# Stacks of split values filled by transfers within SBUF instead of through DRAM

## The chip, the cores and the metric

One core of a Trainium2 chip runs the whole program. The metric is the time of one execution on the device, in microseconds (us), lower is better; several runs are taken and their median stands.

## The reference

x is [16, 128, 256] and ctx_2048 is [16, 128, 256], both float32. Four layers follow each other, each added to x:

```python
x = x + _L0_xattn_ref(_layernorm(x, axis=-1), ctx_2048, ctx_2048)
x = x + _L0_ffn_ref(_layernorm(x, axis=-1), router_w, router_b, expert_w, expert_b)
x = x + _L1_xattn_ref(_layernorm(x, axis=-1), ctx_2048, mask_BxS2_bk0)
x = x + _L1_ffn_ref(_layernorm(x, axis=-1), w_r, b_r, w1, b1, w2, b2)
```

The first layer, which the change is about, cuts the 128 channels of each batch into 8 heads of 16. For each head it takes the 256 x 256 scores qk = q^T k / 4 (a contraction over 16 channels only), a softmax over the last axis, and the product with v, whose 16 channels of the head are the same ctx values as k. The second layer lets each of 16 experts take its 128 best tokens out of 2048 by a softmax of logits. The third is an attention over 128 masked memory tokens; a batch whose mask is all false gives zero. The fourth picks 64 of 128 tokens per batch and puts them through a feed-forward layer.

## The kernel before

Each engine has a program of its own, written out by hand, and they meet only at semaphores. The queue of SP issues nearly all transfers, in its program's order; ACT's queue issues only the small ones of neg_max.

**Units.** The first layer works in eight units (u) of two batches. A unit has 16 steps, one for each batch and head. A step is: scores (L1088 to L1097, PE), the maximum over each row of them (L527 to L532, DVE), the transposed scores with the maximum subtracted inside the product (scores_t, L1099 to L1110, PE), the exponential (L895, ACT), and after every fourth step the product with the values (L1112 to L1125). PE runs scores a good unit ahead of the exponentials: in unit 0 it does all 16 of unit 1 and the first 8 of unit 2. Unit 0's own scores and maxima come before that, from L1160 and L650. The row maxima are transposed (max_t), negated and split in two bf16 parts by ACT (neg_high) and DVE (neg_low), and sent by ACT's queue into two extra rows of q_stack (send_neg_max, L903); scores_t waits for them.

**Splits and stacks.** The scores need float32 accuracy out of bf16 products. So q and k are each split in three bf16 parts (high, mid, low: high is a cast, the rest is subtracted, mid is a cast of the rest, low what remains after it). q_stack and k_stack hold six rows of 16 channels each, with the parts so paired that one product over 96 partitions sums all six part products of a head. There are four slots, one per unit in flight. A stage load (load_stage, L222) brings two batches of ctx and x into ctx_stage and x_stage, 128 channels on 128 partitions. ACT casts (high_k L914, mid_k L920, high_q L924, mid_q L928); for units 0 and 1 DVE subtracts and scales (split_first, L491), for the later ones POOL subtracts (L334 to L350) and DVE scales (scale_q, L484). The head must move from the partition axis to the free axis, and that goes through DRAM: write_k_parts and write_q_parts (L233, L239) write six parts of 128 KB when k_split and q_split say so, and load_stacks (L245) reads them back when all six have landed: three transfers into k_stack and six into q_stack, each of these from 16 rows of 8 KB. PE waits for all nine (stacks_loaded).

**Order on SP** (L274 to L311): stage 0, mask, w_ones (the rows of ones in k_stack, L277), write the parts of 0, stage 1, stacks 0, write the parts of 1, stage 2, stacks 1; then, once the first neg_max has landed, load_x(0) and load_small (ten transfers of small weights); write the parts of 2, stage 3, stacks 2; then by unit: load_x, write parts of u+3, stage u+4, stacks u+3. A stage load waits until the stage before it has been transposed and split. high_k stands between the exponentials in ACT's program: before the first one for unit 2, after the ninth for unit 3, and later after the 14th of unit u for unit u+4.

**Also touched.** DVE computes constants (L508 to L523) after the split of unit 0, and from the mask the row mask_bias (L645) and valid (L646) ahead of the split of unit 1; of all these only high and low are used in the first layer. take_vt (L909) copies the transposed ctx to vt, which the third layer also uses.

## Time and profile before

| what | us |
|---|---|
| median of 3 runs | 420.14 |
| the runs | 419.99, 420.14, 425.96 |
| the profiled execution's own time | 422.43 |
| its span, first to last instruction | 420.2 |

A row of a timeline gives the start of a group of like instructions, the time from the first's start to the last's end, the engine and line, what it writes and reads, how many there are, and in brackets how long the engine had idled before it and who released it. SPq and ACTq are the queues that issue transfers: their time is that of issuing, not of the transfer. GB/s in a window is what all transfers of the core moved in it.

### The profile page before, as it was taken

How to read it: one execution, taken by the hardware profiler on the slowest of the kernel's cores; microseconds unless marked ns; L12 is line 12 of the kernel's file. 1: busy time of each engine (PE TensorE's matmuls, PEld its weight loads, DVE VectorE, ACT ScalarE, POOL GpSimd, SP SyncE). 2: the span in 40 equal slices, each digit the busy share in tenths (PEclk: the TensorE clock that was granted, in tenths of full speed). 3: DMA queues.
4: the chain of work that ended last, by engine and by line, in shares of the span. 5: the costliest groups of instructions: out<-in, count | busy, mean ns of one | idle time of the engine just before them, and what ended most of it. 6: DMA issues, size and time to landing. Idle time of an engine off the chain costs nothing.

```text
span 420.2 us, 7370 instructions
## 1 busy us (share of the span) xinstructions
PE 279.6 (67%) x1872; PEld 182.5 (43%) x1872; DVE 317.7 (76%) x989; ACT 167.6 (40%) x397; POOL 94.8 (23%) x222
## 2 busy tenths in 40 slices
PE   1134777777886877877778621001559999999996
PEld 0011333353442544444334310000438988888884
DVE  5847458899989889799986748888377888787631
ACT  4110543464654536464556500000111566445631
POOL 1101323352415224111111110000133322333200
PEclk9999975789698886899989965555555999999999
DMA  2789388959294581740000380000000000000001
GB/s 88 202 189 153 98 221 187 166 150 165 71 197 79 145 126 54 146 80 1 2 1 2 100 301 0 1 0 2 1 0 0 2 25 25 25 0 25 26 27 51
DMA packets 24379, 32.90 MB, mean 78 GB/s; under 512 B 4066, under 2 KB 22434, under 8 KB 22818
## 3 DMA queue, kind: packets, MB, share of 16 engines
q1 hardware_dynamic: 23842, 32.48, 33.5%
q10 hardware_dynamic: 512, 0.13, 0.2%
q8 instruction: 10, 0.16, 0.2%
q14 instruction: 15, 0.12, 0.1%
HBM read 24.02 MB, written 8.39 MB: 77 GB/s over the span
## 4 chain that ended last, share of the span: by engine, by line
DVE 35%; PE 33%; issue 12%; DMA 8%; ACT 4%; POOL 3%; SPq 2%; DVEq 1%; ACTq 1%; POOLq 0%
DVE row_max L531 7%; PE t_bank L1355 5%; PE pv_bank L1273 5%; PE pv_bank L1121 4%; DMA q_stack<-q_parts_dram 4%; DVE denom_inv L549 3%; PE score_bank L1094 3%; PE scoret_bank L1107 3%; PE t_bank L1150 2%; PE score_bank L1336 2%; DMA q_parts_dram<-q_parts 2%; ACT probs L895 2%; DMA q_stack<-neg_max 2%; PE score_bank L1303 2%; DVE junk L705 1%
## 5 line engine op out<-in xcount | busy, mean ns | idle before, releaser
L895 ACT ACTIVATE probs<-scoret_bank 128x512 f32<-128x512 f32 x128 | 73.1, 596 | 52.5 <-PE scoret_bank L1107 42.3
L531 DVE TENSOR_REDUCE row_max<-score_bank 128x2 f32<-128x512 f32 x112 | 74.4, 679 | 24.3 <-PE score_bank L1094 23.1
L1107 PE MATMUL scoret_bank<-q_stack,k_stack 98*128 98x256 bf16 (+1 forms) x256 | 54.6, 301 | 28.1 <-ACT probs L895 18.7
L1094 PE MATMUL score_bank<-k_stack,q_stack 96*128 96x256 bf16 (+1 forms) x240 | 53.6, 314 | 19.1 <-DMA q_stack<-q_parts_dram 11.0
L355 POOL TENSOR_SCALAR var_eps<-mv 128x1 f32<-128x1 f32 x48 | 9.2, 192 | 189.5 <-DVE mv L567 106.9
L1107 PEld LDWEIGHTS scoret_bank<-q_stack,k_stack 98*128 98x128 bf16 (+1 forms) x256 | 24.2, 104 | 46.6 <-ACT probs L895 20.5
L1121 PE MATMUL pv_bank<-probs,values_ones 128*32 128x256 f32 x512 | 42.0, 455 | 1.0 <-ACT probs L895 1.0
L1094 PEld LDWEIGHTS score_bank<-k_stack,q_stack 96*128 96x128 bf16 (+1 forms) x240 | 21.7, 105 | 47.8 <-issue 15.3
L1273 PE MATMUL pv_bank<-q_stack,k_stack 128*128 (+1 forms) x256 | 36.0, 285 | 0.4 <-ACT q_stack L1070 0.4
L1045 ACT COPY xnt<-score_bank 128x256 f32<-128x256 f32 x16 | 6.0, 373 | 74.6 <-PE score_bank L1294 74.6
L1273 PEld LDWEIGHTS pv_bank<-q_stack,k_stack 128*128 128x128 f32 x256 | 33.9, 202 | 1.3 <-issue 0.9
L1355 PE MATMUL t_bank<-k_stack,probs 128*128 128x256 f32 x128 | 29.4, 382 | 0.0
L357 POOL TENSOR_TENSOR rstd<-var_eps,minus_half 128x1 f32<-128x1 f32 x48 | 26.1, 543 | 8.8 <-POOL var_eps L355 8.8
L549 DVE RECIPROCAL denom_inv<-denom 128x256 f32<-128x256 f32 x16 | 27.7, 1732 | 0.0
L1355 PEld LDWEIGHTS t_bank<-k_stack,probs 128*128 128x128 f32 x128 | 23.7, 190 | 2.9
L1254 PE MATMUL t_bank<-count,same_expert 128*128 128x3 bf16 x15 | 2.8, 187 | 31.4 <-DVE equal L705 31.4
L1150 PE MATMUL t_bank<-wr_moving,xnt 128*128 128x272 f32 x64 | 22.0, 474 | 1.2 <-ACT xnt L943 1.2
L1064 ACT ACTIVATE probs<-pv_bank,b1s 128x128 f32<-128x128 f32 x64 | 17.6, 379 | 11.8 <-PE pv_bank L1273 11.7
L1121 PEld LDWEIGHTS pv_bank<-probs,values_ones 128*32 128x32 f32 x512 | 15.0, 122 | 16.2 <-issue 9.0
L1144 PE MATMUL t_bank<-ident,xn 128*128 128x128 f32 x32 | 7.0, 303 | 18.5 <-DVE xn L573 10.2
L1137 PE MATMUL t_bank<-ident,ctx_stage 128*128 128x128 f32 x32 | 7.6, 383 | 16.3 <-DMA x_stage<-in_x_dram 16.3
L1150 PEld LDWEIGHTS t_bank<-wr_moving,xnt 128*128 128x128 f32 x64 | 13.4, 234 | 8.1 <-issue 4.1
(182 smaller groups left out, 534.5 us busy)
## 6 DMA issues: line engine op xcount, KB each, us to landing
q_stack<-q_parts_dram SPq DMA_DIRECT2D x48, 128.0 KB, 6.9
k_parts_dram<-k_parts SPq DMA_DIRECT2D x24, 128.0 KB
q_parts_dram<-q_parts SPq DMA_DIRECT2D x24, 128.0 KB
k_stack<-k_parts_dram SPq DMA_DIRECT2D x8, 384.0 KB, 4.6
ctx_stage<-in_ctx_dram SPq DMA_DIRECT2D x8, 256.0 KB, 3.2
x_stage<-in_x_dram SPq DMA_DIRECT2D x8, 256.0 KB, 3.9
k_stack<-k_parts_dram SPq DMA_DIRECT2D x8, 256.0 KB, 5.3
xs<-in_x_dram SPq DMA_DIRECT2D x8, 256.0 KB, 7.3
```

The source lines that it names most:

```text
L355: pool.tensor_scalar(work, variance, EPS, factor, ALU.add, ALU.mult).then_inc(s[summed], 1)
L357: pool.tensor_tensor(dst, work, minus_half[:, 0:dst.shape[1]], ALU.pow).then_inc(s[ready], 1)
L531: dve.tensor_reduce(row_max[:, i, :, h], score_bank[bank_of][:, :].rearrange("p (m n) -> p m n", m=2), AX.X, ALU.max).then_inc(s["max_done ...
L549: dve.reciprocal(denom_inv[:, i, :], denom[:, i, :]).then_inc(s["div_step"], 1)
L895: act.activation(probs[:, j % PROBS, :], scoret_bank[j % 2][:, :], ACT.Exp).then_inc(s["exp_done"], 1)
L1064: act.activation(hid[:, h, :], hid_bank[h // 4][:, (h % 4) * P:(h % 4 + 1) * P], ACT.Gelu_apprx_tanh, bias=b1s[:, h:h + 1]).then_inc(s["f_ ...
L1094: ins = pe.matmul(to[:, m * D:(m + 1) * D], q_stack[0:QROWS, slot, h, b_in, m * P:(m + 1) * P], k_stack[0:QROWS, slot, h, b_in, :], start= ...
L1107: ins = pe.matmul(scoret_bank[j % 2][:, k * D:(k + 1) * D], k_stack[0:SROWS, slot, h, b_in, k * P:(k + 1) * P], q_stack[0:SROWS, slot, h, ...
L1121: ins = pe.matmul(pv_bank[i][pair * Q:(pair + 1) * Q, odd * D:(odd + 1) * D], values_ones[:, i, k, pair, odd, :], probs[:, (j - GROUP + 1 ...
L1150: ins = pe.matmul(t1_bank[:, 0:D + NE], xnt[:, i, k, :], wr_moving[:, k, :], start=(k == 0), stop=(k == 1))
L1273: ins = pe.matmul(hid_bank[h // 4][:, (h % 4) * P:(h % 4 + 1) * P], w1s[:, k, h * P:(h + 1) * P], zg[:, k, bass.ds(P * t, P)], start=(k == ...
L1355: ins = pe.matmul(y_bank[:, 0:D], hid[:, h, :], w2s[:, h, :], start=(h == 0), stop=(h == NF - 1))
```

## The change

It takes the two DRAM tensors out. A stage load now puts channel h * 16 + d on partition d * 8 + h (x_split, ctx_split), so that eight neighbouring partitions hold the eight heads of one d. A part on 128 partitions can then be copied to 16 partitions by 8 heads in the order in which both are walked. Each part goes to its place in the stack by a transfer of 128 KB within SBUF: six into k_stack (stack_k) and six into q_stack (stack_q), each group as soon as its part is ready (k_high, k_mid, k_split and so on) instead of after all. A stage load is now four transfers of 128 KB instead of two of 256 KB.

Unit 1 gets its own stage and part buffers, laid over the first six slots of probs, the tile of the exponentials; so stage 1 is loaded right behind stage 0, and ACT waits, before its first exponential, for all that still reads them. DVE's split of units 0 and 1 is cut in pieces: stats_q(1) goes into the split of unit 0, rest_k(1) and scale_q(1) follow the constants, and low_k(1), rest_q(1) and low_q(1) stand between the first five maxima. Unit 1's ctx transposes move behind PE's second score step.

Of the rest: the mask is loaded after the stacks of unit 1; mask_bias is computed by ACT after the exponential of the logits; valid by DVE in the third layer, after the first two c_scale; eight of the constants become more_constants, behind the subtraction of the logits' maxima. take_vt writes vt in channel order, a copy with a stride.

Left out below: the helpers that choose the buffer for unit 1 (ctx_staged, x_staged, k_parts_of, q_parts_of), the same waits on high_q, and POOL's waits for unit 1's splits ahead of unit 2's.

```diff
-        q_parts_dram = nc.dram_tensor("q_parts_dram", (NU, 3, C, NH, 2 * D), BF16, kind="Internal").ap()
-        k_parts_dram = nc.dram_tensor("k_parts_dram", (NU, 3, C, NH, 2 * D), BF16, kind="Internal").ap()
...
+        ctx_stage1 = probs[:, 0, :].rearrange("p (b n) -> p b n", b=2)
+        x_stage1 = probs[:, 1, :].rearrange("p (b n) -> p b n", b=2)
+        k_parts1 = probs[:, 2:4, :].rearrange("p s n -> p (s n)").bitcast(BF16)[:, 0:6 * D].rearrange("p (a n) -> p a n", a=3)
+        q_parts1 = probs[:, 4:6, :].rearrange("p s n -> p (s n)").bitcast(BF16)[:, 0:6 * D].rearrange("p (a n) -> p a n", a=3)
...
+        def wait_staged(eng, u):
+            if is_n(u, 0) or is_n(u, 1):
+                eng.wait_ge(s["staged1" if u else "staged"], 64)
+            else:
+                eng.wait_ge(s["staged"], 64 * u)
...
+            x_split = x.rearrange("b (h d) n -> d h b n", h=NH)
+            ctx_split = ctx_2048.rearrange("b (h d) n -> d h b n", h=NH)
+
             def load_stage(u):
-                if not is_first(u):
-                    sp.wait_ge(s["ctx_t"], u)
-                    sp.wait_ge(s["k_split"], u)
-                    sp.wait_ge(s["q_split"], u)
-                sp.dma_start(ctx_stage[:, :, :], ctx_rows[:, bass.ds(2 * u, 2), :]).then_inc(s["staged"], 16)
-                sp.dma_start(x_stage[:, :, :], x_rows[:, bass.ds(2 * u, 2), :]).then_inc(s["staged"], 16)
+                if not is_first(u) and not is_n(u, 1):
+                    before = 1 if is_n(u, 2) else u
+                    sp.wait_ge(s["ctx_t"], before)
+                    sp.wait_ge(s["k_split"], before)
+                    sp.wait_ge(s["q_split"], before)
+                signal = s["staged1" if is_n(u, 1) else "staged"]
+                for i in range(2):
+                    sp.dma_start(ctx_staged(u)[:, i, :], ctx_split[:, :, bass.ds(2 * u + i, 1), :]).then_inc(signal, 16)
+                for i in range(2):
+                    sp.dma_start(x_staged(u)[:, i, :], x_split[:, :, bass.ds(2 * u + i, 1), :]).then_inc(signal, 16)
...
-            def write_k_parts(u):
-                sp.wait_ge(s["k_split"], u + 1)
-                for part in range(3):
-                    sp.dma_start(k_parts_dram[u, part].rearrange("d h n -> h d n"),
-                                 k_parts[:, part, :]).then_inc(s["parts_written"], 16)
...
-            def load_stacks(u, reused):
-                slot = u % SLOTS
-                wait_apart(sp, s["parts_written"], 96 * (u + 1))
...
+            def stack_k(u, reused):
+                rows = k_stack[:, u % SLOTS].rearrange("p h b n -> p h (b n)")
                 if not is_first(u):
-                    wait_apart(sp, s["stacks_loaded"], 144 * u)
+                    wait_apart(sp, s["k_stacked"], 96 * u)
                 if reused:
                     wait_apart(sp, s["scorest_ready"], STEPS * (u - SLOTS + 1))
-                k_rows = k_parts_dram[u].rearrange("p d h n -> (p d) (h n)")
-                q_rows = q_parts_dram[u].rearrange("p d h n -> p d (h n)")
-                part_of_row = (0, 0, 0, 1, 1, 2)
-                k_to = k_stack[:, slot].rearrange("p h b n -> p (h b n)")
-                q_to = q_stack[:, slot].rearrange("p h b n -> p (h b n)")
-                sp.dma_start(k_to[0:3 * C], k_rows).then_inc(s["stacks_loaded"], 16)
-                sp.dma_start(k_to[3 * C:5 * C], k_rows[0:2 * C]).then_inc(s["stacks_loaded"], 16)
-                sp.dma_start(k_to[5 * C:6 * C], k_rows[0:C]).then_inc(s["stacks_loaded"], 16)
-                for row in range(6):
-                    sp.dma_start(q_to[row * C:(row + 1) * C], q_rows[part_of_row[row]]).then_inc(s["stacks_loaded"], 16)
+                for part, signal, places in ((0, "k_high", (0, 3, 5)), (1, "k_mid", (1, 4)), (2, "k_split", (2,))):
+                    wait_apart(sp, s[signal], u + 1)
+                    for n in places:
+                        sp.dma_start(rows[n * C:(n + 1) * C], k_parts_of(u)[:, part, :]).then_inc(s["k_stacked"], 16)
+
+            def stack_q(u):
+                rows = q_stack[:, u % SLOTS].rearrange("p h b n -> p h (b n)")
+                if not is_first(u):
+                    wait_apart(sp, s["q_stacked"], 96 * u)
+                for part, signal, places in ((0, "q_high", (0, 1, 2)), (1, "q_mid", (3, 4)), (2, "q_split", (5,))):
+                    wait_apart(sp, s[signal], u + 1)
+                    for n in places:
+                        sp.dma_start(rows[n * C:(n + 1) * C], q_parts_of(u)[:, part, :]).then_inc(s["q_stacked"], 16)
...
             load_stage(0)
-            sp.dma_start(mask_u8[:, :, :], mask.rearrange("(a b) m -> a b m", a=1).to_broadcast([P, NB, P])).then_inc(s["mask_loaded"], 16)
+            load_stage(1)
             sp.wait_ge(s["ones_done"], 1)
             sp.dma_start(k_stack[QROWS:SROWS].rearrange("p s h b n -> p (s h) (b n)"),
                          ones_bf[:, :].unsqueeze(1).to_broadcast([2, SLOTS * NH, 2 * D])).then_inc(s["w_ones"], 16)
-            write_k_parts(0)
-            write_q_parts(0)
-            load_stage(1)
-            load_stacks(0, False)
-            write_k_parts(1)
-            write_q_parts(1)
+            stack_k(0, False)
+            stack_q(0)
             load_stage(2)
-            load_stacks(1, False)
+            stack_k(1, False)
+            stack_q(1)
+            sp.dma_start(mask_u8[:, :, :], mask.rearrange("(a b) m -> a b m", a=1).to_broadcast([P, NB, P])).then_inc(s["mask_loaded"], 16)
             sp.wait_ge(neg_loaded[0], 32)
             load_x(0)
             load_small()
 
-            write_k_parts(2)
-            write_q_parts(2)
+            stack_k(2, False)
+            stack_q(2)
             load_stage(3)
-            load_stacks(2, False)
...
             stats_q(0)
-            split_first(0)
+            rest_k(0)
+            dve.tensor_copy(ident_bf[:, :], ident[:, :])
             link(dve.tensor_scalar(earlier[:, :], free_f[:, :], part_f[:, 0:1], None, ALU.is_lt))
-            dve.tensor_copy(ident_bf[:, :], ident[:, :])
-            link(dve.tensor_scalar(work_i[:, :], free_i[:, :], 15, None, ALU.bitwise_and))
+            scale_q(0)
+            low_k(0)
+            rest_q(0)
+            stats_q(1)
+            low_q(0)
             link(dve.tensor_scalar(work_p[:, 0:1], part_i[:, :], 15, None, ALU.bitwise_and))
             link(dve.tensor_scalar(work_p[:, 1:2], part_i[:, :], 4, None, ALU.logical_shift_right))
-            dve.tensor_copy(free_lo[:, :], work_i[:, :])
             dve.tensor_copy(part_lo[:, :], work_p[:, 0:1])
             link(dve.tensor_scalar(half_i[:, :], work_p[:, 1:2], 1, None, ALU.bitwise_and))
             link(dve.tensor_copy(high[:, :], half_i[:, :]))
             dve.tensor_scalar(low[:, :], high[:, :], -1.0, 1.0, ALU.mult, ALU.add)
-            link(dve.tensor_copy(part_hi[:, :], work_p[:, 1:2]))
-            link(dve.tensor_scalar(work_i[:, :], free_i[:, :], 4, None, ALU.logical_shift_right))
-            link(dve.tensor_copy(free_hi[:, :], work_i[:, :]))
-            dve.tensor_scalar(batch_of[:, :], free_f[:, 0:NH], part_hi[:, 0:1], None, ALU.is_equal)
-            link(dve.tensor_scalar(same_expert[:, :], free_lo[:, :], part_lo[:, 0:1], None, ALU.is_equal))
-            link(dve.scalar_tensor_tensor(earlier_batch[:, :], free_hi[:, :], part_hi[:, 0:1], same_expert[:, :],
-                                          ALU.is_gt, ALU.mult))
-            n_consts = k[0]
...
-            dve.wait_ge(s["mask_loaded"], 16)
-
-            dve.tensor_scalar(mask_bias[:, :, :], mask_u8[0:1, :, :], -1.0, -MASKED, ALU.add, ALU.mult)
-            dve.tensor_reduce(valid[:, :], mask_u8[:, :, :], AX.X, ALU.max)
-            stats_q(1)
-            split_first(1)
-
-            def first_maxima(i, q):
-                for j in range(4):
-                    dve.wait_ge(s["scores_ready"], NH * i + 4 * q + j + 1)
-                    dve.tensor_reduce(row_max[:, i, :, 2 * j + q],
-                                      first_score_bank[j][:, :].rearrange("p (m n) -> p m n", m=2),
-                                      AX.X, ALU.max).then_inc(s["max_done"], 1)
-
-            with dve.Fori(0, NH // 4) as q:
-                first_maxima(0, q)
-            first_maxima(1, 0)
+            def first_maximum(n):
+                dve.wait_ge(s["scores_ready"], n + 1)
+                dve.tensor_reduce(row_max[:, n // NH, :, HEADS[n % NH]],
+                                  first_score_bank[n % 4][:, :].rearrange("p (m n) -> p m n", m=2),
+                                  AX.X, ALU.max).then_inc(s["max_done"], 1)
+
+            first_maximum(0)
+            low_k(1)
+            first_maximum(1)
+            first_maximum(2)
+            rest_q(1)
+            first_maximum(3)
+            first_maximum(4)
+            low_q(1)
+            for n in range(5, NH + 2):
+                first_maximum(n)
             neg_low(0, 0)
-            first_maxima(1, 1)
+            for n in range(NH + 2, STEPS):
+                first_maximum(n)
             stats_q(2)
...
+            more_constants()
...
+            dve.tensor_reduce(valid[:, :], mask_u8[:, :, :], AX.X, ALU.max)
             turn(0, True, False, False, False, True)
...
-                act.copy(vt[:, bass.ds(2 * u, 2), :, :].rearrange("p b k c -> p (b k c)"),
-                         t0_bank[:, :]).then_inc(s["vt_done"], 1)
+                act.copy(vt[:, bass.ds(2 * u, 2), :, :].rearrange("p b k (h d) -> p (b k) d h", h=NH),
+                         t0_bank[:, :].rearrange("p (a d h) -> p a d h", a=4, h=NH)).then_inc(s["vt_done"], 1)
 
             def high_k(u):
-                if not is_first(u):
-                    act.wait_ge(s["parts_written"], 96 * u)
-                act.wait_ge(s["staged"], 32 * (u + 1))
-                act.copy(k_parts[:, 0, :], ctx_stage[:, :, :].rearrange("p b n -> p (b n)")).then_inc(s["k_high"], 1)
+                if not is_first(u) and not is_n(u, 1):
+                    act.wait_ge(s["k_stacked"], 96 if is_n(u, 2) else 96 * u)
+                wait_staged(act, u)
...
             high_k(0)
             mid_k(0)
-            take_vt(0)
             high_q(0)
             mid_q(0)
             high_k(1)
             mid_k(1)
-            take_vt(1)
+            take_vt(0)
             high_q(1)
             mid_q(1)
+            take_vt(1)
             neg_high(0, 0, 0)
             send_neg_max(0, 0)
             high_k(2)
+
+            act.wait_ge(s["ctx_t"], 2)
+            act.wait_ge(s["k_split"], 2)
+            act.wait_ge(s["q_split"], 2)
+            act.wait_ge(s["k_stacked"], 96 * 2)
+            act.wait_ge(s["q_stacked"], 96 * 2)
...
+            act.wait_ge(s["mask_loaded"], 16)
+            act.activation(mask_bias[:, :, :], mask_u8[0:1, :, :], ACT.Copy, bias=MASKED, scale=-MASKED).then_inc(s["mask_biased"], 1)
...
-            pe.wait_ge(s["vt_done"], 1)
-            ctx_t(1)
-            pe.wait_ge(s["stacks_loaded"], 144)
+            pe.wait_ge(s["k_stacked"], 96)
+            pe.wait_ge(s["q_stacked"], 96)
             for step in range(STEPS):
+                if step == 2:
+                    pe.wait_ge(s["vt_done"], 1)
+                    ctx_t(1)
                 scores(first_score_bank[step % 4], 0, step // NH, HEADS[step % NH], step - 3)
```

## Rows read from the trace of the kernel before

**Rows 1.** Page, busy time, share of the span and instructions of each engine.

```profile
PE 279.6 (67%) x1872; PEld 182.5 (43%) x1872; DVE 317.7 (76%) x989; ACT 167.6 (40%) x397; POOL 94.8 (23%) x222
```

**Rows 2.** Chain that ended last, in order: start us, us, what.

```profile
1.24 3.13 DMA x_stage<-in_x_dram
...
11.99 3.96 DMA q_parts_dram<-q_parts
...
19.68 7.59 DMA q_stack<-q_parts_dram
...
37.02 6.49 DMA q_stack<-neg_max
```

**Rows 3.** Timeline to T: start us, us, engine, line, what [idle before].

```profile
2.66 0.90 SPq L277 DMA_DIRECT2D k_stack<-ones_bf  x1
...
8.55 1.96 SPq L236 DMA_DIRECT2D k_parts_dram<-k_parts  x3
...
9.98 0.69 DVE L504 TENSOR_TENSOR q_parts<-q_rest,q_parts 128x512 bf16<-128x512 f32 x1 [0.68 <-ACT q_parts L930]
...
27.32 1.04 PE L1094 MATMUL score_bank<-k_stack,q_stack 96*128 96x256 bf16 x4 [8.81 <-DMA q_stack<-q_parts_dram]
```

**Rows 4.** Timeline from T to E.

```profile
35.70 1.98 ACTq L906 DMA_DIRECT2D q_stack<-neg_max  x2
...
44.27 0.60 ACT L895 ACTIVATE probs<-scoret_bank 128x512 f32<-128x512 f32 x1 [5.87 <-PE scoret_bank L1107]
```

**Rows 5.** Timeline of unit 0.

```profile
49.06 1.95 SPq L236 DMA_DIRECT2D k_parts_dram<-k_parts  x3
...
59.19 0.62 ACT L918 CAST k_parts<-ctx_stage 128x512 bf16<-128x512 f32 x1 [4.59 <-DMA x_stage<-in_x_dram]
...
68.89 1.04 PE L1094 MATMUL score_bank<-k_stack,q_stack 96*128 96x256 bf16 x4 [2.15 <-DMA q_stack<-q_parts_dram]
```

**Rows 6.** Windows: stretch, us, busy us by engine, granted clock, DMA share, GB/s.

```profile
20.50:25.50 5.00, 0.00 (x0) 0.00 (x0) 2.31 (x4) 1.24 (x2) 0.15 (x1) 1.00 1.05 162
35.50:41.50 6.00, 0.51 (x2) 0.03 (x2) 3.46 (x9) 0.62 (x1) 2.04 (x3) 1.00 1.01 148
5.00:6.50 1.50, 0.59 (x3) 0.19 (x1) 1.05 (x4) 0.29 (x2) 0.50 (x2) 1.00 0.14 30
43.60:77.00 33.40, 26.19 (x154) 12.37 (x158) 23.32 (x45) 14.85 (x30) 10.99 (x16) 0.71 0.75 179
```

**Rows 7.** Page, DMA issues: out<-in, queue, count, KB each, us to landing.

```profile
q_stack<-in_ctx_dram SPq DMA_DIRECT2D x1, 2048.0 KB, 8.3
...
wr_moving<-in_L_ffn_expert_w_dram SPq DMA_DIRECT2D x2, 128.0 KB, 2.6
```

**Rows 8.** Timeline of unit 2.

```profile
103.87 0.59 ACT L895 ACTIVATE probs<-scoret_bank 128x512 f32<-128x512 f32 x1
...
112.60 2.03 SPq L242 DMA_DIRECT2D q_parts_dram<-q_parts  x3
...
123.02 0.62 ACT L918 CAST k_parts<-ctx_stage 128x512 bf16<-128x512 f32 x1
```

**Rows 9.** Timeline, constants and mask at the start, and where they go.

```profile
12.32 0.14 DVE L518 CAST part_hi<-work_p 128x1 f32<-128x1 int32 x1
...
13.48 0.35 DVE L523 SCALAR_TENSOR_TENSOR earlier_batch<-free_hi,part_hi,same_expert 128x128 bf16<-128x128 f32 x1
...
15.01 2.27 DVE L646 TENSOR_REDUCE valid<-mask_u 128x16 f32<-128x2048 uint8 x1
...
251.99 0.42 DVE L686 TENSOR_REDUCE lg_sum<-logits 128x16 f32<-128x256 f32 x1 [0.48 <-ACT logits L1037]
...
299.11 0.37 ACT L1045 COPY xnt<-score_bank 128x256 f32<-128x256 f32 x1 [47.15 <-PE score_bank L1294]
...
301.18 0.29 DVE L781 TENSOR_REDUCE sc_max<-score_bank 128x1 f32<-128x128 f32 x1 [1.85 <-PE score_bank L1305]
```

More of the change, by code:

```diff
@@ L239, in write_q_parts @@
-            def write_q_parts(u):
-                sp.wait_ge(s["q_split"], u + 1)
-                for part in range(3):
-                    sp.dma_start(q_parts_dram[u, part].rearrange("d h n -> h d n"),
-                                 q_parts[:, part, :]).then_inc(s["parts_written"], 16)
-            def load_stacks(u, reused):
-                slot = u % SLOTS
-                wait_apart(sp, s["parts_written"], 96 * (u + 1))
+            def stack_k(u, reused):
+                rows = k_stack[:, u % SLOTS].rearrange("p h b n -> p h (b n)")
@@ L502, in split_first, with low_q @@
                                   ALU.subtract).then_inc(s["q_rest"], 1)
+            def low_q(u):
                 dve.wait_ge(s["q_mid"], u + 1)
[L504 removed]
+                dve.tensor_tensor(q_parts_of(u)[:, 2, :], q_rest[:, :], q_parts_of(u)[:, 1, :],
+                                  ALU.subtract).then_inc(s["q_split"], 1)
             stats_q(0)
[L507 removed]
+            rest_k(0)
```

75 lines of the change are left out of this document (51 added, 24 removed).

## Prediction

> **What bounds the kernel now.** I read the page first, then the chain of waits in order of time, the timelines of the first 45 us and of one unit in the middle, and the rates of a few windows. DVE is busy 76% of the span and PE 67% [rows 1], so no engine is full, and what a change of transfers is worth has to be read from the waits. The chain shows them: 3.13 us for the first stage load, 3.96 us for the write of the q parts to DRAM, 7.59 us for the last read into the q stack, 6.49 us for the row of maxima [rows 2]. Thus the first scores start at 27.32 us, after PE idled 8.81 us, though the last split ended at 10.67 us [rows 3]. The first exponential starts at 44.27 us [rows 4]. Call these two instants T and E. In unit 0 one more read of a stack is waited for: 2.15 us of PE at 68.89 us; and ACT idles 4.59 us for stage 3, until 59.19 us, which is E+14.9 [rows 5]. After that no stack is late. So the change can earn only in T, in E and at those two waits, all before 77 us.
>
> **What a 128 KB transfer into 16 partitions costs (d).** Everything hangs on d, the distance at which such transfers follow each other. Before, the q stack takes six of them from DRAM per unit, in pieces of 8 KB; after, all twelve are of this kind, in pieces of 1 KB, out of SBUF. The only SBUF to SBUF copy of before in pieces of 1 KB is w_ones: alone in its window, into two neighbouring partitions, it moved 30 GB/s [rows 6]. The nearest rows are the two windows in which almost only q reads move: 162 and 148 GB/s with the DMA engines 101 to 105% busy [rows 6], so 131 KB take 0.81 and 0.885 us. SP needs 0.65 us to issue one with a permuted side (1.96 us for three, [rows 3]); that is the lower end, for then SP is the limit. I take 0.81, since the destination is the same and the DMA engines, not SP, were the limit there. The upper end is 1.1: if four neighbours together take no more than the two of w_ones did, sixteen take 120 GB/s. 0.81 is the nearer row, of the same sixteen rows and the same sequence of them.
>
> The Trainium skill (SBUF — State Buffer, section "Door 1: The DMA port swizzle") says that the rate depends on how many of 16 SBUF ports the partitions reach; sixteen neighbours reach four of them, which by its figure per port would be 109 GB/s, an estimate of 1.2 us per transfer; the sum below would then be +5.6 instead of -7.7, and the time 425.7 us. The trace does not bear it out for the reads of before, 148 to 162 GB/s into such rows [rows 6], so I leave it as a chance: it is rival B's mechanism with a somewhat higher price.
>
> **Step 1, T.** Stage 0 is now four transfers of 128 KB, each issued in about 0.63 us: the fourth starts at 2.6 and, with 2.6 us to land [rows 7], is there at 5.2 us instead of 4.37: +0.8. The split chain is otherwise that of before; stats_q(1) inside it costs 0.2 beyond a gap that was there. Last split at 11.7 instead of 10.67. SP issues eight stage loads (to 5.8) and w_ones (0.90, [rows 3]), so the first stack transfer is issued at 6.6; twelve at 0.65 take SP to 14.4, and each part is ready before its turn. The write to DRAM and its landing go. A transfer lands some 3.0 us after its issue (between 2.6 for 128 KB in [rows 7] and 3.96 in [rows 2]). T = 6.6 + 3.0 + 11d = 18.5, 8.8 us earlier.
>
> **Step 2, E.** DMA: stage 2 (512 KB, 2.1 us at the pace of 2048 KB in 8.3 [rows 7]), twelve transfers of unit 1 and the mask (1.0) queue behind stack 0, and drain at (T-1) + 2.1 + 12d + 1.0 = 30.3. DVE: the maxima of before went out 8.4 us after T (35.70, [rows 4]); now three subtractions of unit 1 stand between them (2.1), two maxima fewer come ahead, but the eighth must still have been transposed: T+9.7 = 28.2. Behind low_k(1) and low_q(1) on DVE wait only the maxima, paid here. Before, the negated maxima were issued at 35.70 and landed at 43.5, two us after the window in which the reads ended [rows 2, 6]; so now they land at 30.3 + 2.0 = 32.3, and E = 33.1. The added ACT waits on both stacks of unit 1 are over by then (about 31.3). Gain: 44.27 - 33.1 = 11.2.
>
> **Step 3, unit 0.** SP first issues load_x(0) and the small weights, 5.5 us as before (43.5 to 49.06, [rows 5]), from E-0.8 to E+4.7. Then it has twelve stack transfers instead of six writes before stage 3. They land at E+4.7+3.0+11d = E+16.6, stage 3 follows in 2.1: E+18.7, against E+14.9. high_k(3) stands in ACT's program between the exponentials, and PE waits for these: +3.8. In return stack 2 is there at E+16.6, long before its use at E+24.6: -2.15. Net +1.65.
>
> **Step 4, later units: 0.** In unit 2, which begins at 103.87, q_split comes at 112.6 and high_k needs the next stage at 123.02 [rows 8]. Five k transfers now go at once at the start, the last q one by U+10 and the four stage loads by U+12, landing at U+14.5, against a need at U+19.15: 4.6 us of cover; without it ACT would pay whatever is late. The strided take_vt is bounded by 0 and by once more a 0.6 us instruction per unit, beside an ACT that is 40% busy: 0.
>
> **Step 5, constants and mask.** Eight constants move behind the subtraction of the logits. Six of them ran from 12.32 to 13.83, with the other two 2.0 us; 0.48 us of it fits where DVE waited for ACT's exponential [rows 9]: +1.5, in the open. The reduction of the mask to valid is 2.27 us, set where DVE idled 1.85 us for the scores [rows 9]: 0.42, of which the second batch's later maximum hides a part: +0.3. mask_bias goes to an ACT that then idles 47.15 us [rows 9]: 0. Their leaving the beginning is in step 1 and 2 already, where DVE had been idle.
>
> **Sum.** -11.2 + 1.65 + 1.5 + 0.3 = -7.7. The profiled execution took 422.43, so 414.7; the median of the runs shown is 420.14, 2.3 lower, and I carry the difference: 412.4 us. In d the whole is 34d - 35.2 (12 and 11 transfers in step 2, 11 in step 3).
>
> **Rivals.**
> *A, SP is the limit.* For it: SBUF to SBUF leaves out DRAM, and SP issues only each 0.65 us. Against: engines full at 0.81. Then T = 16.75; unit 1's last transfer is issued at 24.8, the maxima go out at 26.4 and land at 29.4; E = 30.2, -14.1. Stage 3 lands at E+4.7+7.8+1.95+2.6 = E+17.05, +2.15 against the 2.15 saved. With 1.8 for step 5: -12.3, and 407.8 us.
> *B, slower.* Transfers into 16 partitions follow each other at 1.1 us: T = 21.7, E = 39.8 (-4.5), stage 3 at E+21.9 (+7.0 - 2.15), step 5 +1.8: +2.2, 422.3 us. What ACT loses at high_k(3) then exceeds all that E gained; the sign turns at d = 1.04. For it: the 30 GB/s of w_ones, pieces of 1 KB and twice as many such transfers. Against: 0.81 to 0.885 measured with the same destinations.
> *C, the clock takes it back.* In 43.6 to 77 us PE had a mean granted clock of 0.71 [rows 6]: half speed for over half of it. With ACT held to E+18.7, PE idles longer and may get 1.2 GHz for all of the rest, some 18 us; PE was busy 26 of 33 us there, so its later half, 13 us, would grow by a good third, of which the other engines hide a little: +4. -3.7, and 416.4 us.
> That the change does not do what it says I leave aside: the diff takes out both DRAM tensors.
>
> **Numbers.** Forecast 42%, A 33%, C 15%, B 10%. A measurement can tell about 2%, 8.4 us, from no change; that line is 411.7, almost on the forecast. Faster by over 2%: nearly all of A and a third of the forecast, 0.45. Slower by over 2% (above 428.5) needs B and more on top: 0.05. The same: 0.50. The range reaches from A with its spread to a little beyond C, 405 to 420; B is left out.
>
> **What would show it.** Right: first scores at 18 to 19 us, first exponential near 33, ACT idle for stage 3 some 3 to 4 us longer, no PE wait for stack 2, a unit of some 26 us from unit 1 on, and DVE's constants at the logits 2 us. Windows full of stack transfers at 160 GB/s speak for d = 0.81, 200 for A, 120 for B. Wrong: E later than 37, a wait for a stack or a stage in the later units, or ACT's strided copy well above 0.6 us.

## The result, and the profile after

The changed kernel takes 428.12 us (median of four, 423.78 to 428.77); the kernel before, beside it, 420.06 us. The ratio is 1.018 [1.009, 1.027]: slower by some 8 us, where 412.4 us (405 to 420) was forecast; whether it is by more than 2%, the interval leaves open. One of the four executions of the kernel before, 425.96 us, fell in a slower state of the chip and is not in the ratio. The profiled execution took 428.44 us with a span of 426.7, against 422.43 and 420.2.

The page of the changed kernel, its first part, the DMA totals and the two stack groups of the DMA issues:

```profile
span 426.7 us, 7366 instructions
...
PE 281.9 (66%) x1872; PEld 184.6 (43%) x1872; DVE 315.6 (74%) x988; ACT 172.5 (40%) x398; POOL 94.5 (22%) x222
...
DMA packets 29244, 26.62 MB, mean 62 GB/s; under 512 B 4322, under 2 KB 28834, under 8 KB 29218
...
HBM read 11.43 MB, written 2.10 MB: 32 GB/s over the span
...
k_stack<-k_parts SPq DMA_DIRECT2D x42, 128.0 KB, 4.0
q_stack<-q_parts SPq DMA_DIRECT2D x42, 128.0 KB, 5.0
```

The engines do nearly what they did [rows 1]; the traffic over the DRAM tensors is gone and less is moved in all (26.62 MB, before 32.90). So the loss is in waits. The chain of waits up to 55 us (answers to [rows 2]):

```profile
7.68 1.85 SPq L270
15.64 7.48 DMA q_stack<-q_parts
...
33.86 4.32 DMA q_stack<-neg_max
54.65 8.12 DMA x_stage<-in_x_dram
```

The write to DRAM is gone and the row of maxima is waited for 4.32 us instead of 6.49, but the stack is still waited for 7.48 us, and a new item is longer than any of before: 8.12 us for a stage load in unit 0. The timeline up to the first exponential (answers to [rows 3, 4]):

```profile
5.96 0.87 SPq L295 DMA_DIRECT2D k_stack<-ones_bf  x1
6.97 5.23 SPq L270 DMA_DIRECT2D k_stack<-k_parts  x6
12.32 3.90 SPq L279 DMA_DIRECT2D q_stack<-q_parts  x6
...
23.25 1.01 PE L1137 MATMUL score_bank<-k_stack,q_stack 96*128 96x256 bf16 x4 [16.81 <-DMA q_stack<-q_parts]
...
39.02 0.60 ACT L928 ACTIVATE probs<-scoret_bank 128x512 f32<-128x512 f32 x1 [3.78 <-PE scoret_bank L1150]
```

SP has issued the last transfer of stack 0 at 16.2 us, but the first scores (T) wait for it until 23.25: 7.0 us, where the forecast had 4.1 (18.5 after 14.4). T comes 4.1 us earlier than before and the first exponential (E) 5.25 us. The timeline of unit 0 (answers to [rows 5]):

```profile
43.89 4.41 SPq L270 DMA_DIRECT2D k_stack<-k_parts  x6
48.49 4.12 SPq L279 DMA_DIRECT2D q_stack<-q_parts  x6
52.72 1.24 SPq L254 DMA_DIRECT2D ctx_stage<-in_ctx_dram  x2
54.02 1.23 SPq L256 DMA_DIRECT2D x_stage<-in_x_dram  x2
...
62.85 0.62 ACT L951 CAST k_parts<-ctx_stage 128x512 bf16<-128x512 f32 x1 [12.26 <-DMA x_stage<-in_x_dram]
...
64.02 0.61 PE L1150 MATMUL scoret_bank<-q_stack,k_stack 98*128 98x256 bf16 x2 [10.46 <-ACT probs L928]
```

ACT stands 12.26 us for stage 3, which comes at E+23.8 (before E+14.9), and PE stands 10.46 us because the next exponential is behind that cast. PE's wait for stack 2 is gone. The windows (stretch, us, busy us of PE, PEld, DVE, ACT, POOL, granted clock, DMA share, GB/s), the first full of stack transfers, the second unit 0:

```profile
13.00:22.00 9.00, 0.00 (x0) 0.00 (x0) 0.98 (x3) 1.96 (x3) 0.52 (x2) 1.00 1.15 123
39.00:79.30 40.30, 25.18 (x156) 12.34 (x158) 22.98 (x45) 15.83 (x31) 10.95 (x16) 0.67 0.90 132
```

123 GB/s are 1.07 us per 128 KB (131 KB by 123), with the DMA engines full. How long transfers took from issue to landing (the last figure of a row) in two short stretches of the changed kernel: the first stack transfer of unit 0, issued at 6.97; then the first of unit 2, issued at 43.89, and the last of the small weights ahead of it:

```profile
k_stack<-k_parts SPq DMA_DIRECT2D x1, 128.0 KB, 4.7
...
k_stack<-k_parts SPq DMA_DIRECT2D x1, 128.0 KB, 6.0
...
b1s<-in_L_ffn_b_dram SPq DMA_DIRECT2D x1, 4.0 KB, 6.0
```

Both stack transfers had been given 3.0 us to land. From these on the twelve of stack 0 landed 1.04 us apart (11.71 to 23.12), those of stack 2 1.02 apart (49.89 to 61.14). Where the 6.5 us of span come from, by the start of the first exponential of each unit in the timelines (unit 7 up to the start of its last one):

| stretch | before | after | difference |
|---|---|---|---|
| start to E | 44.3 | 39.0 | -5.3 |
| unit 0 | 32.8 | 40.3 | +7.5 |
| units 1 to 6 | 146.4 | 147.7 | +1.3 |
| unit 7 | 14.0 | 15.6 | +1.6 |
| constants at the logits | 0.5 | 1.9 | +1.4 |
| the rest | 182.2 | 182.2 | 0.0 |

### The profile page after: what moved, and what is told of

It reads as the page before. It is cut to its first block, busy times and chain, and to the rows that moved or that the text cites. A ratio compares the mean times of both kernels' runs of the same rounds, so it can differ in the third digit from the quotient of the medians.

```text
span 426.7 us, 7366 instructions
## 1 busy us (share of the span) xinstructions
PE 281.9 (66%) x1872; PEld 184.6 (43%) x1872; DVE 315.6 (74%) x988; ACT 172.5 (40%) x398; POOL 94.5 (22%) x222
## 2 busy tenths in 40 slices
DMA packets 29244, 26.62 MB, mean 62 GB/s; under 512 B 4322, under 2 KB 28834, under 8 KB 29218
## 4 chain that ended last, share of the span: by engine, by line
DVE 35%; PE 34%; issue 12%; SPq 7%; DMA 5%; ACT 3%; POOL 2%; DVEq 1%; ACTq 0%; POOLq 0%
DVE row_max L563 7%; PE t_bank L1403 5%; PE pv_bank L1319 5%; PE pv_bank L1164 5%; PE t_bank L1193 3%; DVE denom_inv L581 3%; PE scoret_bank L1150 3%; PE score_bank L1137 2%; SPq L270 2%; PE score_bank L1384 2%; DMA x_stage<-in_x_dram 2%; DMA q_stack<-q_parts 2%; SPq L279 2%; ACT probs L928 2%; PE score_bank L1351 1%
## 5 line engine op out<-in xcount | busy, mean ns | idle before, releaser
L1150 PE MATMUL scoret_bank<-q_stack,k_stack 98*128 98x256 bf16 (+1 forms) x256 | 55.3, 305 | 32.8 <-ACT probs L928 27.1
L1137 PEld LDWEIGHTS score_bank<-k_stack,q_stack 96*128 96x128 bf16 (+1 forms) x240 | 22.2, 107 | 54.4 <-issue 31.5
L1319 PEld LDWEIGHTS pv_bank<-q_stack,k_stack 128*128 128x128 f32 x256 | 33.9, 202 | 1.3 <-issue 0.9
L1193 PE MATMUL t_bank<-wr_moving,xnt 128*128 128x272 f32 x64 | 23.4, 498 | 1.3 <-ACT xnt L978 1.3
L1187 PE MATMUL t_bank<-ident,xn 128*128 128x128 f32 x32 | 7.3, 313 | 18.5 <-DVE xn L605 10.7
L352 POOL TENSOR_TENSOR k_rest<-ctx_stage,k_parts 128x512 f32<-128x512 f32 x6 | 6.9, 1153 | 40.3 <-ACT k_parts L951 40.3
```

The source lines that it names most:

```text
L1137: ins = pe.matmul(to[:, m * D:(m + 1) * D], q_stack[0:QROWS, slot, h, b_in, m * P:(m + 1) * P], k_stack[0:QROWS, slot, h, b_in, :], start= ...
L1150: ins = pe.matmul(scoret_bank[j % 2][:, k * D:(k + 1) * D], k_stack[0:SROWS, slot, h, b_in, k * P:(k + 1) * P], q_stack[0:SROWS, slot, h, ...
L1193: ins = pe.matmul(t1_bank[:, 0:D + NE], xnt[:, i, k, :], wr_moving[:, k, :], start=(k == 0), stop=(k == 1))
L1319: ins = pe.matmul(hid_bank[h // 4][:, (h % 4) * P:(h % 4 + 1) * P], w1s[:, k, h * P:(h + 1) * P], zg[:, k, bass.ds(P * t, P)], start=(k == ...
```

## The experiments

The figures are medians of several executions where none else is named. Two theories stood at first. *P*: sixteen neighbouring partitions are a slow destination, whatever the source and the size of the pieces. *S*: the pieces of 1 KB are what is slow.

**The transfers alone.** A kernel that computes nothing of the reference and only moves data, section after section, each of up to twelve transfers of 128 KB, waited for at its end (`order` is that of the changed kernel's stack rows; one execution):

```diff
+section(0, [(near[n * C:(n + 1) * C, s], src[:, s, :]) for s, n in order])
+section(1, [(near[n:6 * C:6, s], src[:, s, :]) for s, n in order])
+section(2, [(near[n * C:(n + 1) * C, s], src[:, s, :]) for s in range(2) for n in (0, 2)])
+section(3, [(near[n * C:(n + 1) * C, s], x[s].rearrange("(h d) n -> d h n", h=NH)) for s, n in order])
+section(4, [(near[n * C:(n + 1) * C, s].rearrange("p h n -> p (h n)"), wide[n * C:(n + 1) * C].rearrange("p h n -> p (h n)")) for s, n in order])
+section(5, [(flat[:, j, :], src[:, j % 2, :]) for j in range(12)])
+section(6, [(near[n * C:(n + 1) * C, s].rearrange("p h n -> p (h n)"), x[s].rearrange("(d h) n -> d (h n)", h=NH)) for s, n in order])
```

> This kernel computes nothing of the reference: it only moves blocks of 128 KB, twelve in a row (four in section 2), each section waiting for the one before. Sections: 0 SBUF to SBUF, 1 KB pieces, into 16 neighbouring partitions, in the order of the changed kernel; 1 the same pieces into 16 partitions six apart; 2 four copies as in 0, but all into rows 0 and 2; 3 DRAM to 16 neighbours, 1 KB pieces; 4 SBUF to SBUF, 8 KB pieces, 16 neighbours on both sides; 5 SBUF to SBUF, 1 KB pieces, 128 partitions on both sides; 6 DRAM to 16 neighbours, 8 KB pieces, as the kernel before. Theory P (the destination's 16 neighbouring partitions take only so much): 0 at 120 to 130 GB/s, 2 and 3 and 4 no faster than that, 1 and 5 at 200 or more, where SP's issue of 0.65 us is the limit. Theory S (the 1 KB pieces are slow): 4 and 6 at 150 or more, 0, 1, 3 and 5 all near 120. Theory R (SBUF as the source is slow): 3 and 6 at 150 or more, 0, 1, 4, 5 near 120.

Its windows (stretch, us, busy us of POOL, granted clock, DMA share, GB/s), one per section, 0 to 6 in order:

```profile
9.00:21.60 12.60, 0.00 (x0) 1.00 1.07 125
24.20:32.10 7.90, 0.00 (x0) 1.00 0.72 199
33.70:38.00 4.30, 0.00 (x0) 1.00 0.94 122
40.30:52.30 12.00, 0.00 (x0) 1.00 1.09 131
54.80:65.40 10.60, 0.00 (x0) 1.00 0.95 148
67.70:75.30 7.60, 0.00 (x0) 1.00 0.62 207
76.60:88.50 11.90, 0.00 (x0) 1.00 0.99 133
```

Section 0 is the changed kernel's own pattern: 12.6 us for twelve, 1.05 us each, 125 GB/s. The same bytes into rows six partitions apart (section 1) take 0.66, which is SP's issue time, with the DMA engines 72% busy. From DRAM into neighbours they take 1.00 (section 3) and, in pieces of 8 KB as before, 0.99 (section 6). Pieces of 8 KB within SBUF into neighbours take 0.88 (section 4), four transfers into stack rows 0 and 2 alone 1.07 each (section 2), and copies from all partitions to all partitions 0.63 (section 5). So P holds; the size of the pieces is worth 0.17 us at most (section 4 also reads from 16 neighbours instead of 128 partitions, so that the two are not told apart), the source 0.05.

**The distance of the rows.** Sections of twelve transfers, each into the same 16 partitions 1, 2, 3, 4, 6 and 8 apart; nothing of the reference is computed (one execution):

```diff
+for number, step in enumerate((1, 2, 3, 4, 6, 8)):
+    for j in range(12):
+        sp.dma_start(near[0:15 * step + 1:step, j], src[:, j % 2, :]).then_inc(moved[number], 16)
+    sp.wait_ge(moved[number], 16 * 12)
```

> Computes nothing of the reference: six sections of twelve copies, each 128 KB from 128 partitions in pieces of 1 KB into 16 partitions of SBUF, that lie 1, 2, 3, 4, 6 and 8 apart; every copy of a section writes the same 16 partitions. Theory P, a limit of the groups of partitions that the 16 reach: 1 apart about 1.05 us per copy or a little more, since here no two copies go to different rows; all the others near SP's 0.65, because 16 partitions two apart already reach twice as many groups. If instead the distance itself counted, the time would fall step by step from 1 to 8.

Its windows, in the order of the distances:

```profile
4.80:19.50 14.70, 0.00 (x0) 1.00 1.10 107
22.40:30.20 7.80, 0.00 (x0) 1.00 0.73 201
31.80:43.80 12.00, 0.00 (x0) 1.00 1.06 131
46.40:54.30 7.90, 0.00 (x0) 1.00 0.73 198
56.00:63.80 7.80, 0.00 (x0) 1.00 0.73 202
65.40:73.40 8.00, 0.00 (x0) 1.00 0.74 197
```

All into the same neighbours: 1.22 us each. 2, 4, 6 and 8 apart: 0.65, SP's limit. 3 apart: 1.00, which had not been expected. The Trainium skill (SBUF — State Buffer, section "Door 1: The DMA port swizzle") gives the port of each partition: blocks of four, those 32 apart on one port. By that table sixteen neighbours put four partitions on each of four ports, distances 2, 4, 6 and 8 put at most two on any, and distance 3 puts three on some. By its 27 GB/s per port the fullest port would take an estimated 1.2, 0.6 and 0.9 us for its 32, 16 and 24 KB; the runs show 1.22, no more than 0.65, and 1.00. The runs agree with it in order and roughly in size, if one counts the fullest port and not the number of ports reached: by the table distances 2, 3, 4 and 8 all reach eight ports, and only 3 is slow.

A section's mean holds its faster start. Three stretches from the middle, of the same partitions and of distance 3 in this run, and of section 0 of the run before:

```profile
8.00:18.00 10.00, 0.00 (x0) 1.00 1.16 101
34.00:42.00 8.00, 0.00 (x0) 1.00 1.16 123
...
12.00:20.00 8.00, 0.00 (x0) 1.00 1.15 118
```

These are 1.30, 1.07 and 1.11 us each: for the same neighbours and for distance 3 some 8 and 19% more than the estimates of 1.2 and 0.9.

**The stacks spread** (channel d of stack row n goes to partition 6d+n instead of 16n+d, in both stacks, so that the products are the same):

```diff
-sp.dma_start(rows[n * C:(n + 1) * C], k_parts_of(u)[:, part, :]).then_inc(s["k_stacked"], 16)
+sp.dma_start(k_stack[n:QROWS:6, u % SLOTS].rearrange("p h b n -> p h (b n)"), k_parts_of(u)[:, part, :]).then_inc(s["k_stacked"], 16)
...
-sp.dma_start(rows[n * C:(n + 1) * C], q_parts_of(u)[:, part, :]).then_inc(s["q_stacked"], 16)
+sp.dma_start(q_stack[n:QROWS:6, u % SLOTS].rearrange("p h b n -> p h (b n)"), q_parts_of(u)[:, part, :]).then_inc(s["q_stacked"], 16)
```

> The changed kernel with one thing altered: channel d of stack row n lies on partition 6d + n instead of 16n + d in both stacks, so that the same 16 pieces groups go to partitions six apart. The products over 96 partitions are the same sums in another order. Theory P: a stack transfer costs SP's 0.65 us, first scores at about 17 to 18 us, first exponential at 30 to 32 (39.0 in the changed kernel), stage 3 lands some 17 us after that instead of 23.8, so the time falls by 14 to 18 us against the changed kernel, to 411 to 415. Theories S and R: no move, 426 to 428.

415.07 us, ratio to the kernel before 0.985 [0.977, 0.993]; 13 us less than the changed kernel. Its timeline:

```profile
18.40 1.01 PE L1135 MATMUL score_bank<-k_stack,q_stack 96*128 96x256 bf16 x4 [11.92 <-DMA q_stack<-q_parts]
...
31.70 0.60 ACT L926 ACTIVATE probs<-scoret_bank 128x512 f32<-128x512 f32 x1 [1.31 <-PE scoret_bank L1148]
...
51.33 0.62 ACT L949 CAST k_parts<-ctx_stage 128x512 bf16<-128x512 f32 x1 [7.89 <-DMA x_stage<-in_x_dram]
```

T is 18.40, E 31.7, stage 3 at E+19.6. With d = 0.65, as spread rows take alone, the forecast's formulas (those of rival A) give 16.75, 30.2 and E+17.05: each is too early, by 1.65, 1.5 and 2.6 us. The first stack transfers of units 0 and 2 landed 4.3 and 4.9 us after their issue here, for the 3.0 of the formulas; that is most of what T and stage 3 are late by. So P's price is the larger part of what the change lost, but not all.

**The small weights behind stage 3.** In the changed kernel SP issues load_x(0) and the small weights from 38.2 to 43.7 us, ahead of stack 2 and stage 3:

```diff
-            load_x(0)
-            load_small()
...
             load_stage(3)
+            load_x(0)
+            load_small()
```

> The changed kernel with load_x(0) and load_small behind the stage load of unit 3 in SP's program. If what unit 0 pays is that stage 3 comes late because of all that SP issues and the queues carry ahead of it, stage 3 lands 4 to 5 us earlier after the first exponential and the time falls by 3 to 5 us, to 423 to 425. If stage 3 is not what unit 0 waits for, the time stays within 1 us of 428.

422.22 us, 5.9 less than the changed kernel, ratio to before 1.004 [1.000, 1.009]. E stays at 38.9; ACT's wait falls from 12.26 to 5.51 us, and unit 0 from 40.3 to 34.2 us:

```profile
56.64 0.62 ACT L950 CAST k_parts<-ctx_stage 128x512 bf16<-128x512 f32 x1 [5.51 <-DMA x_stage<-in_x_dram]
```

What unit 0 pays is thus set by what stands ahead of stage 3 in SP's queue. The first stack transfer of unit 2 now lands 3.3 us after its issue instead of 6.0.

**The constants back at the beginning:**

```diff
+            more_constants()
...
-            more_constants()
```

> The changed kernel with the eight constants of more_constants computed where DVE waits for the first scores. My account puts their cost at the logits at 1.4 us and their cost at the start at nothing, since DVE idles 9.9 us there: about 1.4 us less between the logits' subtraction and the sum of the exponentials, the first scores where they were. A rival: something else waits there (ACT's exponential or its new mask work), then DVE idles as long as the constants took, and nothing is gained.

One execution, 424.19 us. At the logits the sum now follows the exponential at once:

```profile
253.73 0.42 ACT L1078 ACTIVATE logits<-logits 128x256 f32<-128x256 f32 x1 [3.72 <-DVE logits L715]
...
254.18 0.42 DVE L718 TENSOR_REDUCE lg_sum<-logits 128x16 f32<-128x256 f32 x1 [0.48 <-ACT logits L1078]
```

From the end of the subtraction to the sum it is 0.49 us, in the changed kernel 1.86 (256.69 to 258.55): 1.4 us for the move, and E (38.8) gives nothing back. The rest of the 4 us lies in units 1 to 7, within what these differ between executions; the total of one execution tells nothing here, as the changed kernel's own four reach down to 423.78.

**w_ones ahead of stage 1**, to free SP for the first stack transfers; the chain of the changed kernel has 1.85 us of SP there:

```diff
-            load_stage(1)
...
+            load_stage(1)
```

> The changed kernel with the transfer of w_ones ahead of stage 1 instead of behind it. In the changed kernel it is issued right before the first stack transfer, writes 64 pieces of 1 KB to two partitions, at about 25 GB/s in the profile's DMA line, and SP needs 5.2 us for the first six stack transfers instead of 3.9. If it holds up the engines that carry it, the first scores come 1 to 1.5 us earlier (23.25 to about 22) and the six transfers are issued in about 4 us. If the gap is only the wait for the k parts, nothing moves.

One execution, 427.14 us, and T at 23.06 (before the edit 23.25). The first six stack issues shrink from 5.23 to 4.01 us, but SP now stalls at stage 1 (2.43 us for two issues, 1.24 in the changed kernel), and nothing comes earlier: the first stack transfer, issued at 8.17 instead of 6.97, lands at 11.53 instead of 11.71, and the others 1.04 us apart behind it. The same transfers are still ahead of it, in another order. So the stall on the chain was not what T waited for; that was the landing of the first transfer and eleven times d.

**All four edits together:**

> The changed kernel with spread rows (e2), small weights after stage 3 (e3), constants early (e4) and w_ones early (e5) together. If the four costs add up: first scores near 17, first exponential near 30.5, unit 0 some 4 us shorter than in e2 (36.1), 415.07 - 4 - 1.4 - 1.3 = 408 to 409 us, ratio to the kernel before 0.970 to 0.975. If the small weights cost nothing once the transfers are fast: 412.

407.62 us, ratio to before 0.973 [0.966, 0.979]. The savings on the changed kernel, 13.1, 5.9 and 1.4 us, add up to 407.8 (the expectation had put w_ones at 1.3 more and the small weights at 4). The six executions range from 403.43 to 411.8, and the profiled one is the fastest: T is 18.09, E 31.5, unit 0 31.0 us, and units 1 to 6 take 142.5 us, 5 less than in the changed kernel. That the sum comes out to 0.2 us is therefore partly luck.

```profile
46.09 0.62 ACT L948 CAST k_parts<-ctx_stage 128x512 bf16<-128x512 f32 x1 [4.10 <-DMA x_stage<-in_x_dram]
```

**Stage 3 between the k and the q transfers of unit 2**, on top of the four, against the wait that is left:

```diff
-            def load_stage(u):
+            def load_stage(u, x_taken="q_split"):
...
-                    sp.wait_ge(s["q_split"], before)
+                    sp.wait_ge(s[x_taken], before)
...
+            load_stage(3, "q_ready")
...
-            load_stage(3)
```

> As e6, but stage 3 is loaded between the k and the q transfers of unit 2 (its x may be overwritten once q is scaled, so the wait is on q_ready). If unit 0 still waits for stage 3 behind the six q transfers, stage 3 lands 3 to 4 us earlier and the time is 2 to 3 us under e6. Rival: SP now waits for the transposes of unit 2's ctx before it may issue the q transfers, stack 2 has slack, and unit 0 is bound by PE and DVE by then: no difference to e6.

413.23 us, ratio 0.982 [0.977, 0.987]: 5.6 us worse than the four. Stage 3 is there at 45.85 instead of 46.09, for SP could issue it only from 40.51 (before the edit 40.92): what holds it is the buffer, not the queue. The q transfers now wait in SP behind it, from 35.71 to 44.11 us, and all that follows with them, so that stage 4 is late (ACT waits 6.31 us at 70.43) and unit 1 takes 28.5 us instead of 21.45. The 2 to 3 us expected as a gain did not come. The same miss as in the change itself: a transfer moved forward is paid by the one behind it.

**The kernel before, with its stacks spread**, still over DRAM, k in six reads of 128 KB instead of three larger ones (the counts waited for, 144 and now 192, are left out):

```diff
-                sp.dma_start(k_to[0:3 * C], k_rows).then_inc(s["stacks_loaded"], 16)
-                sp.dma_start(k_to[3 * C:5 * C], k_rows[0:2 * C]).then_inc(s["stacks_loaded"], 16)
-                sp.dma_start(k_to[5 * C:6 * C], k_rows[0:C]).then_inc(s["stacks_loaded"], 16)
+                for row, part in enumerate((0, 1, 2, 0, 1, 0)):
+                    sp.dma_start(k_stack[row:QROWS:6, slot].rearrange("p h b n -> p (h b n)"), k_rows[part * C:(part + 1) * C]).then_inc(s["stacks_loaded"], 16)
...
-                    sp.dma_start(q_to[row * C:(row + 1) * C], q_rows[part_of_row[row]]).then_inc(s["stacks_loaded"], 16)
+                    sp.dma_start(q_stack[row:QROWS:6, slot].rearrange("p h b n -> p (h b n)"), q_rows[part_of_row[row]]).then_inc(s["stacks_loaded"], 16)
```

> The kernel before, through DRAM, with the same spread of the stack rows over partitions six apart; k takes six transfers of 128 KB instead of three. Theory P says that its reads too wait for the 16 neighbours: twelve reads at SP's 0.42 us from 16.04 on give first scores near 24.3 instead of 27.3, the first exponential 3 us or more earlier, and the second stack wait of unit 0 gone: 3 to 6 us faster than before, 414 to 417. If DRAM was its limit: no gain, and a us of SP's time lost.

414.99 us, ratio 0.987 [0.983, 0.991], as fast as the changed kernel with the same spread:

```profile
25.04 1.03 PE L1093 MATMUL score_bank<-k_stack,q_stack 96*128 96x256 bf16 x4 [6.97 <-DMA q_stack<-q_parts_dram]
```

T is 2.3 us earlier than in [rows 3], E 6.4. So the reads of before paid for their neighbours too (that k now comes in six reads was not tried by itself), and the change with nothing but its destination mended is not measurably faster than this: E comes at 31.7 instead of 37.9 us, and unit 0 (36.1 against 33.9), the constants and the later units take it back.

**The same kernel with its small weights behind unit 2:**

```diff
-            load_x(0)
-            load_small()
...
+            load_x(0)
+            load_small()
```

> The kernel before, through DRAM, with the spread rows of e8 and, as in e3, load_x(0) and the small weights behind unit 2's stage load and stacks. What is left between this and e6 is what leaving DRAM is worth. If DRAM costs what step 1 and 2 said (the write, its landing, the order of the splits), e6 stays 4 to 6 us ahead: 412 to 414 here, unit 0 near 31 to 32 us, first exponential unchanged at 38. If the spread and the order were all there was to gain, this comes to 408.

420.91 us, ratio 1.001 [0.999, 1.003], 6 us worse than without the edit. Unit 0 stays (34.1 us), since there stage 3 waits for the splits, q_split at 49.8 us, and not for SP. In unit 1 the small weights stand ahead of unit 3's parts, which are issued at 69.49 instead of 62.51, and stage 4 is waited for 4.74 us at 79.34. The edit that gives 5.9 us in the changed kernel costs 6 here, and neither of the expected times, 412 to 414 or 408, was met. The best kernel over DRAM is thus at 414.99 us and the best without it at 407.62; no other order over DRAM was tried, so that these 7 us are not shown to be what leaving DRAM is worth.

## Why the prediction was wrong

**What a 128 KB transfer costs (d): this step failed.** 0.81 us was taken, 1.05 to 1.07 is what such transfers took, in the kernel (123 GB/s) and alone (125 GB/s), and 1.22 all into the same sixteen; the 120 GB/s named as the sign of B were what the windows showed. The reading of the two windows [rows 6] was right. The last read of k landed at 22.45 us, the six of q after it 0.66 to 0.85 us apart, and the rate stays at 154 GB/s, 0.85 us each, where almost only these are left:

```profile
22.00:25.50 3.50, 0.00 (x0) 0.00 (x0) 0.89 (x2) 0.62 (x1) 0.00 (x0) 1.00 1.01 154
```

What failed is the step from these reads to the copies that replace them, "since the destination is the same". Reads of that kind took 0.99 us when they ran alone (section 6), copies in pieces of 1 KB 1.05. Why the reads were faster in the kernel than alone no run shows. The Trainium skill's port rule, which spoke against the choice, was set aside on these windows; it was right about the destination, and too high for changing groups.

**Steps 1 and 2.** The stage load (at 5.2 us), the last split (11.86, forecast 11.7) and SP's issues (to 16.2 against 14.4) were about right, and with d = 1.05 the formula of step 2 gives E = 38.65, measured 39.02. T was 2.1 us later than its formula has it with d = 1.05 (21.15), and 1.65 later with spread rows. The term that was too small is the 3.0 us from issue to landing: the first stack transfer was issued 0.4 us later than forecast, and landed 4.7 us after that, behind stage 1 and w_ones. That E is met all the same is luck: the row of maxima was to land 2.0 us behind all transfers. Before, it landed at 43.51, 0.4 us behind the last read (43.11), and now at 38.18, with the last stack transfer of unit 1 down at 37.41.

**Step 3.** The mechanism was right: stage 3 late behind twelve transfers, PE's wait for stack 2 gone. With d = 1.05 the formula gives E+21.35, measured E+23.8, 2.5 us more. With spread rows it is 2.6 more than the formula has, so this part does not hang on d. It is again the 3.0 us to landing: the first stack transfer of unit 2 stood behind the small weights, the last of which itself took 6.0 us to land, and landed 6.0 us after its issue, 3.0 more than allowed; the issue was 0.2 later than forecast, and the eleven steps and the stage behind them took 0.7 less. Unit 0 lost 8.9 us by stage 3, won 2.15 and lost 0.75 elsewhere: +7.5, where +1.65 stood. Of the 5.85 missed, d makes 2.65 (11 by 0.24), stage 3's own term 2.45, the rest 0.75. That the small weights ahead of the stacks cost 5.5 us was right: their move gave 6.1 of unit 0.

**Step 4** held for its waits but one: in unit 2 the next stage is there in time and ACT casts without idling (at 125.72), and PE waits for no later stack. In unit 1 ACT idles 0.83 us for the next stage:

```profile
100.37 0.62 ACT L951 CAST k_parts<-ctx_stage 128x512 bf16<-128x512 f32 x1 [0.83 <-DMA x_stage<-in_x_dram]
```

The copy of take_vt takes 1.00 us instead of 0.58. That is well above 0.6, one of the prediction's signs of being wrong; the 0.4 us more per unit lie within its bound of 0.6, and what they cost in time no run takes apart. Units 1 to 7 are 2.9 us longer in the profiled pair; as the four runs with one edit each range over as much (units 1 to 6 146.2 to 148.9 us, unit 7 14.0 to 15.7), this stays unattributed.

**Step 5.** The constants cost 1.4 us (1.5 forecast, and their return gained it), the reduction of the mask nothing (0.3).

**The sum.** With d = 1.05, 34d-35.2 is +0.5; stage 3 adds 2.5, the rest of unit 0 0.75, E 0.4, the later units 2.9, step 5 takes 0.4: 6.6, for a measured 6.5 between the spans. Of the 14.2 us from the forecast's -7.7 to the measured 6.5, d makes 8.2 (34 by 0.24) and the time to landing at stage 3 2.5. By the estimate from the Trainium skill's price, 1.2 us, the sum was +5.6 and the time 425.7, near the 428.12; partly by luck, as the real d was lower and other terms higher.

**Rivals.** B was the mechanism, given 10% and 422.3 us. Its turning point, d = 1.04, is next to the measured price of 1.05; what took the kernel to the slow side was stage 3. A has its d of 0.65 with spread rows alone, and gave 407.8 us for what then took 415.07. C did not happen: after stage 3's wait is taken out, 0.75 us of unit 0 is left for it, and the mean granted clock of PE behind that wait was no lower than in the last stretch of unit 0 before, 0.61 against 0.56:

```profile
64.00:79.30 15.30, 13.04 (x74) 6.15 (x78) 14.39 (x29) 6.87 (x15) 6.67 (x11) 0.61 1.03 130
...
59.20:77.00 17.80, 13.59 (x70) 6.14 (x74) 15.71 (x32) 7.60 (x16) 7.05 (x11) 0.56 0.90 190
```

The range left B out, though a row (30 GB/s into two partitions) and the Trainium skill's port rule spoke for it, and against it only windows of another kind of transfer; it should have reached B's 422.3 and the 425.7 of the price above at least.

## What to carry to other kernels

Before planning transfers into a few partitions, count how many of them share a port, by the Trainium skill's table named above, and lay them so that the fullest port has few: here rows six apart were worth 13 us in one kernel and 5.5 in the other, and with that alone the form without DRAM was no faster than the one over it. The price of one kind of transfer is not that of the kind that replaces it: measure the new kind alone before it is multiplied by 34. And give the first transfer of a group the time to landing that transfers have where a queue is full (4.7 and 6.0 us here), not that of an empty one. What is won at the start must be followed to the next thing in the same queue: here 5.25 us won at the first exponential were lost, and more, at one stage load that stood behind the new transfers, and moving a group of small loads gained 5.9 us in one kernel and lost 6 in the other.

## What the runs showed of the hardware

- 128 KB into 16 partitions, each time the same: 1.22 us (107 GB/s) for neighbours, 1.00 for rows 3 apart, 0.65 for 2, 4, 6 or 8 apart, the last being SP's issue time. Into changing groups of neighbours 1.05. In the middle of a section the first two are 1.30 and 1.07, the last 1.11.
- A larger distance is not always the faster one: 2 apart 201 GB/s, 3 apart 131. Distances of 5 and more than 8 were not tried, 7 neither.
- Within SBUF, 1 KB pieces out of 128 partitions take 1.05 us and 8 KB pieces out of 16 neighbours 0.88; DRAM as the source makes 1.00 and 0.99. In the kernel before, such reads of 8 KB pieces landed 0.66 to 0.96 us apart in units 0 and 1; why they were faster there is open.
- The time from issue to landing of the first 128 KB copy of a stack was 6.0 us behind the small weights and 2.3 with these moved away and the rows spread (unit 2 of the changed kernel and of the four edits together).
- ACT's copy of 128x512 with a strided destination took 1.00 us, 0.58 with a plain one.
